# A two-layer transformer on one core: routed experts over all rows, or over sorted tiles of the rows that chose them

## The reference, cut to what matters

```
scores = softmax(x @ gate_w.T)                        # 8 experts
topk_w, topk_i = top_k(scores, 2)
topk_w = topk_w / sum(topk_w)
cw = zeros.at[token, topk_i].add(topk_w)              # 2 of 8 are not zero
g, u = x @ wg[e], x @ wu[e]                           # e of 8, 256 -> 128
eo = (silu(g) * u) @ wd[e]                            # 128 -> 256
y = sum over e of cw[:, e] * eo[e]
shared = (silu(x @ sg) * (x @ su)) @ sd               # 256 -> 256 -> 256
x = layernorm(x + y + shared)
```

## Time and profile before

| | us |
|---|---|
| median of 3 runs (794.51 to 799.8) | 799.59 |
| span of the profiled execution, core 0 | 798.3 |
| second attention's 8 items | 378.6 to 546.9 |
| tail | 546.9 to 798.3 |

### The profile page before, as it was taken

The page is one execution under the profiler, slowest core; times in us unless marked ns, Lnnn a source line. Parts: engine busy times, 40 slices in busy tenths (PEclk is TensorE's granted clock), DMA queues, the critical chain, the costliest instruction groups (busy, mean ns, idle before and its releaser), DMA issues.

```text
span 798.3 us, 10995 instructions
## 1 busy us (share of the span) xinstructions
PE 743.9 (93%) x3831; PEld 332.2 (42%) x3831; DVE 402.3 (50%) x984; ACT 395.3 (50%) x519; POOL 174.3 (22%) x194
## 2 busy tenths in 40 slices
PE   5998889999989789897999999989999999999996
PEld 2656222224323535342222222324466457448345
DVE  1578225334767787965133333465432842652525
ACT  1245858886778153453888888773121130120110
POOL 0012534443232222145244223231200200000000
PEclk9997789999999799999899999999999999999999
DMA  8401242332220000022444555470000000000000
GB/s 278 120 0 30 54 82 37 53 56 37 40 38 1 1 0 14 0 40 49 79 81 82 83 83 83 78 200 1 0 1 0 28 0 1 26 0 0 26 1 27
DMA packets 32276, 36.15 MB, mean 45 GB/s; under 512 B 7956, under 2 KB 21009, under 8 KB 32065
## 3 DMA queue, kind: packets, MB, share of 16 engines
q1 hardware_dynamic: 32217, 35.41, 21.7%
HBM read 12.54 MB, written 2.10 MB: 18 GB/s over the span
## 4 chain that ended last, share of the span: by engine, by line
PE 65%; DVE 13%; SPq 10%; ACT 5%; issue 4%; DMA 2%; POOL 1%; DVEq 0%; ACTq 0%; POOLq 0%
PE ps L2109 17%; PE ps L1303 13%; PE ps L1286 11%; PE ps L2134 9%; ACT probs L1373 3%; SPq L1024 3%; PE ps L1683 3%; SPq L999 2%; SPq L1031 2%; PE ps L400 2%; DVE stats L291 1%; PE ps L649 1%; PE ps L1670 1%; DVE raw L1206 1%; PE ps L2119 1%
## 5 line engine op out<-in xcount | busy, mean ns | idle before, releaser
L1373 ACT ACTIVATE probs<-ps 128x1024 f32<-128x1024 f32 (+1 forms) x320 | 276.0, 965 | 66.2 <-PE ps L1286 66.0
L1286 PE MATMUL ps<-ops_mem 99*128 99x512 bf16 (+3 forms) x768 | 167.5, 340 | 13.5 <-issue 6.7
L1303 PE MATMUL ps<-probs,vstat 128*32 128x512 f32 (+3 forms) x1536 | 168.9, 513 | 9.2 <-DVE raw L1206 7.4
L2109 PE MATMUL ps<-ops_mem,parts_mem 128*128 128x512 f32 x320 | 147.1, 605 | 1.0 <-DVE probs L2161 1.0
L1389 POOL TENSOR_SCALAR_AFFINE_SELECT probs<-probs 128x512 f32<-128x512 f32 x128 | 84.8, 663 | 223.1 <-ACT probs L1373 222.4
L1286 PEld LDWEIGHTS ps<-ops_mem 99*128 99x128 bf16 x768 | 58.1, 99 | 166.5 <-ACT probs L1373 86.1
L1206 DVE COPY raw<-ps 128x512 f32<-128x512 f32 x32 | 22.1, 691 | 167.4 <-PE ps L1303 167.2
L2055 ACT ACTIVATE ops_mem<-ps 128x512 f32<-128x512 f32 x40 | 23.9, 597 | 142.9 <-PE ps L2109 142.9
L2109 PEld LDWEIGHTS ps<-ops_mem,parts_mem 128*128 128x128 f32 x320 | 58.9, 191 | 68.4 <-issue 66.0
L2134 PE MATMUL ps<-parts_mem,probs 128*128 128x256 f32 x320 | 70.5, 380 | 0.0
L2134 PEld LDWEIGHTS ps<-parts_mem,probs 128*128 128x128 f32 x320 | 60.3, 190 | 8.4 <-issue 0.5
(11 more groups left out here) (191 smaller groups left out, 723.6 us busy)
## 6 DMA issues: line engine op xcount, KB each, us to landing
ops_mem<-parts_mem SPq DMA_DIRECT2D x276, 64.0 KB
ops_mem<-parts_mem SPq DMA_DIRECT2D x66, 32.0 KB
yT<-in_xT SPq DMA_DIRECT2D x4, 512.0 KB, 7.9
xres<-in_x SPq DMA_DIRECT2D x1, 2048.0 KB, 14.6
out<-ops_mem SPq DMA_DIRECT2D x3, 512.0 KB, 2.9
rope<-in_rope SPq DMA_DIRECT2D x1, 1024.0 KB, 6.8
parts_mem<-in_wg SPq DMA_DIRECT2D x2, 512.0 KB, 5.0
parts_mem<-in_wu SPq DMA_DIRECT2D x2, 512.0 KB, 6.9
```

What stands on the lines that cost most here:

```text
L1286: last = nc.tensor.matmul(ps[:, bank, o:o + CH - lo], kT[0:KDIM, buf, h if kh == GH else 0, kt * P:(kt + 1) * P], qT[0:KDIM, buf, h, c * C ...
L1303: last = nc.tensor.matmul(ps[32 * h:32 * h + 32, AV, lo:CH], vstat[:, i % 2, kt, h if kh == GH else 0, :], probs[:, s % PRING, h, 0:CH - l ...
L1373: nc.scalar.activation(o, banks, ACT.Exp, scale=score_scale).then_inc(s_exp, 1)
L2109: last = nc.tensor.matmul(ps[:, 4 + 2 * (e % 2) + m, :], w, xT[:, kk, :], start=kk == 0, stop=kk == 1)
```

## The change

Every token chose two experts, so a batch has 2048 (token, choice) pairs. The new tail sorts them by expert into 23 tiles of 128 slots (16 full ones and up to 7 more for the experts' partly filled last tiles), 46 for both batches.

- `Route` takes the place of `FirstChunk` and `Gates`. For a batch it makes the logits, softmax and the two highest, counts by a matmul with a triangle of ones how many earlier pairs chose the same expert (`rank`), and from it each pair's slot (`place`) and each tile's expert (`name_tiles`). For batch 0 (chunks 0 and 1: 4 half projections, 4 half transposes, logits of 8 tiles, rank) this is put beside items 4 to 7 of attention 1, for batch 1 into the first rounds of the tail.
- POOL scatters x to a DRAM tensor by slot: for each of 16 token tiles two indirect DMAs of 128 rows with 1 KB. Those DRAM tensors are filled with zeros during attention 0: after the stackings of items 2 and 3 SP issues a DMA of 3 MB each, from DRAM to DRAM.
- SP loads slot tiles back (ring of 6), PE transposes a tile, multiplies by gate and up weights side by side (256 columns), transposes the product, multiplies by the down weights; the expert's column is a register that PE loads from SBUF (`value_load`). SP stores the tile's result to DRAM, POOL gathers the two results of a token by indirect DMAs (32 in all), and DVE adds them, weighted, to x + shared. Gathers go through a ring of 4 token tiles.
- The tail works in rounds: in round r of a batch PE transposes tile r (`turn_x`), makes gate and up of tile r-1, transposes the product of tile r-2 and makes down of tile r-3; ACT follows with `keep_x(r)`, silu of r-1 and `keep_y(r-3)`, DVE with `keep_hT(r-2)` and `gated(r-1)`. There are 26 rounds in a batch.
- `load(j + 6)` stands behind `store(j)` on SP, which waits for `keep_y(j)`; `gather` waits for all stores of its batch and, from t = 4, for `add_routed(t - 4)`; the last loop over LAST takes tiles (0, 1), (2) and (3) of the last chunk.
- The shared expert is made by chunk, chunks 0 and 1 ahead of the tiles (with projections and transposes of chunks 2 and 3; in the excerpt below up of (1, 1), four half transposes and down of chunk 1 are left out), 2 and 3 at the end.

```diff
@@ attention, PE, DVE, POOL, SP of the second (and SP of the first) @@
+            def beside(self, pe, i, s):
+                if i == NI // 2 and s in (7, 8, 9, 10):
+                    self.project(pe, (s - 7) // 2, (s - 7) % 2)
+                if (i, s) in ((5, 4), (5, 8)):
+                    self.turn(pe, 0, (4, 8).index(s))
+                if (i, s) in ((5, 11), (6, 3)):
+                    self.turn(pe, 1, (11, 3).index(s))
+                if (i, s) == (6, 5):
+                    self.logits(pe, 0)
+                if (i, s) == (7, 2):
+                    self.rank(pe, 0)
+                    if layer == 1 and i == NI // 2:
+                        route.sum(dve, 0, 0)
+                        route.sum(dve, 0, 1)
+                        route.sum(dve, 1, 0)
+                        route.sum(dve, 1, 1)
+                        route.norm(dve, 0)
+                        route.apply(dve, 0)
...
                     take(dve, i, 1)
                 for i in range(2, NI):
                     ops.stack(sp, i)
+                    if layer == 0 and i in (2, 3):
+                        sp.dma_start(slot_x_of[i - 2].rearrange("(j p) n -> p j n", p=P),
+                                     a["none"].rearrange("p (j n) -> p j n", j=1).to_broadcast([P, SLOT_TILES, C])
+                                     ).then_inc(s_fill, 16)
@@ tail, SP @@
+                for b in range(NB):
+                    sp.wait_ge(s_scattered[b], 16 * 2 * TPB)
+                    lo, hi = b * SLOT_TILES, (b + 1) * SLOT_TILES
+                    for j in range(lo, lo + XR):
+                        load(j)
+                    for j in range(lo, hi):
+                        store(j)
+                        if j + XR < hi:
+                            load(j + XR)
@@ tail, POOL @@
+                outputs_there(pool, 2)
+                pool.wait_ge(ops[1].s_scores, NEXP * (NI - 1))
+                route.stage(2)
+                for t in range(TPB):
+                    scatter(t)
+                    if t == 2:
+                        outputs_there(pool)
+                        route.stage(3)
+                for t in range(TPB, 2 * TPB):
+                    scatter(t)
+                for t in range(2 * TPB):
+                    gather(t)
@@ tail, PE @@
+                def gate_up(j):
+                    b, n = j // SLOT_TILES, j % SLOT_TILES
+                    if n == 0:
+                        pe.wait_ge(route.s_tile, b + 1)
+                    at = pe.value_load(expert_of[b][0:1, n:n + 1], min_val=0, max_val=(EXPERTS - 1) * C)
+                    pe.wait_ge(s_xT, j + 1)
+                    for kk in range(2):
+                        last = nc.tensor.matmul(ps[:, bank(j), C:2 * C], slot_xT[:, j % 4, kk * P:(kk + 1) * P],
+                                                wgu[:, kk, bass.ds(at, C)], start=kk == 0, stop=kk == 1)
...
+                shared_up(0, 0)
+                route.project(pe, 2, 0)
+                route.project(pe, 2, 1)
+                shared_up(0, 1)
+                route.project(pe, 3, 0)
+                shared_down(0)
+                route.project(pe, 3, 1)
+                shared_up(1, 0)
...
+                for b in range(NB):
+                    for r, (j, j1, j2, j3) in rounds(b):
+                        if j is not None:
+                            turn_x(j)
+                        if j1 is not None:
+                            at[j1] = gate_up(j1)
+                        if j2 is not None:
+                            turn_h(j2)
+                        if j3 is not None:
+                            down(j3, at[j3])
+                        if (b, r) == (0, 0):
+                            route.logits(pe, 1)
+                        if (b, r) == (0, 7):
+                            route.rank(pe, 1)
+                        if (b, r) == (1, SLOT_TILES):
+                            shared_up(2, 0)
+                        if (b, r) == (1, SLOT_TILES + 1):
+                            shared_up(2, 1)
+                shared_down(2)
+                shared_up(3, 0)
+                shared_up(3, 1)
+                shared_down(3)
@@ tail, ACT @@
+                        if (b, r) == (0, 3):
+                            route.exp(act, 1)
@@ tail, DVE @@
+                        if b == 1 and r >= 8 and r % 2 == 0 and r < 24:
+                            add_routed((r - 8) // 2)
+                        if (b, r) == (1, 15):
+                            end(0, 0)
...
+                end(1, 1)
+                begin(2)
+                shared_gated(3, 0)
+                shared_gated(3, 1)
+                begin(3)
+                for t in range(2 * CT, 3 * CT):
+                    add_routed(t)
+                end(2, 2)
+                for t in range(3 * CT, 4 * CT):
+                    add_routed(t)
                 for n, (lo, hi) in enumerate(LAST):
...
+                    end(3 + n, 3, lo, hi)
```

More of the change, by code:

```diff
@@ L403, in project_y @@
             last.then_inc(s_proj, 1)
[L405 to L425 removed]
+        PICK_COUNT = 19
@@ new lines, in keep_turned, with logits @@
+            def keep_turned(self, eng, copy, m, kk):
+                eng.wait_ge(self.s_turned, 2 * m + kk + 1)
+                if m >= 2:
+                    eng.wait_ge(self.s_yst, NC)
+                copy(chunk_xT[m][:, kk, :], ps[:, self.BANK, :]).then_inc(self.s_xT, 1)
+            def logits(self, pe, b):
+                pe.wait_ge(self.s_xT, 4 * b + 4)
+                for m in range(2):
+                    for t in range(CT):
+                        for kk in range(2):
+                            o = 8 * (CT * m + t)
+                            last = nc.tensor.matmul(ps[:, self.BANK, o:o + 8],
+                                                    chunk_xT[2 * b + m][:, kk, t * P:(t + 1) * P],
+                                                    gatew[:, kk, :], start=kk == 0, stop=kk == 1)
+                last.then_inc(self.s_logit, 1)
@@ new lines, in rank @@
+            def rank(self, pe, b):
+                if b == 0:
+                    pe.wait_ge(self.s_table, 32)
+                pe.wait_ge(self.s_mask, b + 1)
+                nc.tensor.matmul(ps[:, self.BANK, 0:72], before_, mask[:, 0:72], start=True, stop=False)
+                for d in range(1, TPB + 1):
+                    last = nc.tensor.matmul(ps[:, self.BANK, 8 * d:72], ones_, mask[:, 0:72 - 8 * d],
+                                            start=False, stop=d == TPB)
+                last.then_inc(self.s_rank, 1)
@@ L1224, in _ @@
                 for i in range(NI):
-                    if layer == 1 and i == NI - 2:
-                        first.sum(dve)
                     if layer == 0 and i == NI - 1:
@@ L1331, in _ @@
                             ahead.beside(pe, i, s)
[L1332 to L1338 removed]
+                        if layer == 1:
+                            route.beside(pe, i, s)
                     if more:
@@ L1379, in _ @@
                 for i in range(NI):
-                    if layer == 1 and i == NI - 2:
-                        pool.wait_ge(s_y, NI)
-                        pool.wait_ge(s_vstat[layer], NI // 2)
-                        for g in range(NG // 2):
-                            first.stage(g, 0)
                     for d, s in enumerate(DIAG):
@@ new lines, in add_routed @@
+                def add_routed(t):
+                    b, m, n = t // TPB, t // CT, t % TPB
+                    dve.wait_ge(*s_begun(m + 1))
+                    dve.wait_ge(s_back[t % BR], 32 * (t // BR + 1))
+                    w = w_end[:, m, t % CT, :]
+                    for c in range(2):
+                        if c:
+                            dve.wait_ge(*s_sum(2 * t + 1))
+                        vec.scalar_tensor_tensor(out=w, in0=back[:, t % BR, c, :], scalar=gate[b][:, c, n:n + 1], in1=w,
+                                                 op0=ALU.mult, op1=ALU.add).then_inc(s_sum.sem, 1)
@@ L2304 @@
     bf16 = ml_dtypes.bfloat16
-    sel = np.zeros((32, EXPERTS, P), np.float32)
-    for part in range(3):
-        for e in range(EXPERTS):
-            sel[part * EXPERTS + e, e] = 1
     row = np.arange(P)
+    eight = np.arange(EXPERTS)
     perm = np.zeros((P, P), np.float32)
@@ L2355 @@
         "rope": _rope_tables(),
-        "sel": sel.astype(bf16),
+        "none": np.zeros((P, C), np.float32),
+        "before": np.concatenate([row[:, None] < row[None, :], np.ones((P, P), bool)], 1).astype(bf16),
+        "route": np.concatenate([np.tile(P * eight, 8), (eight[None, :] <= eight[:, None]).reshape(-1), np.arange(24)]
+                                ).astype(np.float32)[None],
         "iota8": np.arange(EXPERTS, dtype=np.float32)[None],
```

828 lines of the change are left out of this document (454 added, 374 removed).

## The result

The changed kernel takes 757.92 us (median of 4 runs, 755.33 to 762.57), the kernel before 799.69 beside it: ratio 0.950, 95% interval 0.945 to 0.955. The forecast was 766, range 738 to 806. The profiled execution has a span of 755.6 us.

What follows compares the result with a forecast made beforehand. PE was taken as the bound, busy 93% of the span and the tail its list of matmuls. Tail minus 43, attention plus 9, fill plus 1, together minus 33: span 765, forecast 766 us, range 738 to 806.

Steps and rivals of the forecast that it cites:

- What is removed, and PE's bare work: Tail: 181 of 251 us of expert work go; each slot tile costs PE 1.62 us, 46 of them 75 us.
- The round, 2.1 us: Slot-tile rounds in the tail: PE's work plus waits and register arithmetic, 2.1 us each, range 1.65 to 3.0.
- The four waits at 0.1: In each slot-tile round PE waits at four places, taken at 0.1 us each.
- the load ring: Slot-tile loads behind stores must land two rounds later: round at least 1.7 us with 2.2 landing, 2.35 with 3.5.
- rival 3: PE's clock falls to 1.2 GHz in the rounds: 1.62 us more a round, 840 us in all; chance 0.03.
- Rival 2: Register load not hidden, or dynamic address slows PE's issue: rounds of 3.0 us, 41 more, 807; chance 0.10.
- POOL's indirect DMAs: 64 scatters and gathers, taken at 1.5 us each, the middle between 0.34 to 0.7 and 2.36 us.
- its bounds of 1.67 and 1.8: Time per scatter, in us, up to which scatters stay hidden in the tail's first part and in batch 0.
- the 794: Total in us if POOL paid the page's whole indirect-DMA cost, 2.0 us plus bytes, all 64 times.
- Attention 1, plus 9: Second attention: routing work put beside it lengthens it by 9 us, range 5 to 16.
- it comes 1 to 1.5 us late each, 3.5: Second attention, items 4, 5 and 6: DVE's `take` is late behind queued routing steps, 3.5 us together.
- First part, gap, end, fill: Tail before the first round 34.5 us, gap between batches 3.4, end 47; zero fill in attention 0 plus 1.

Runs made afterwards that it cites:

- e4: Changed kernel with each slot tile's load issued once its buffer is turned, ahead of stores: 767.25 us, 5.5 less than e0.
- e10: Changed kernel with four edits: e3, e5, e4 with its gap fault addressed, and chunk 0's last norm in pieces: 731.48 us, ratio 0.918.
- e1: Changed kernel with each slot tile's expert a program constant, not a register load (wrong experts): 764.65 us, 8.1 less than e0.
- e2: Changed kernel with an added GpSimd addition of 0.62 us behind each of the 64 indirect DMAs: 772.87 us, ratio 0.968.
- e7: Changed kernel with the first batch's routing moved from the second attention to the start of the tail: 782.86 us, ratio 0.982.
- e11: Kernel of e10 with the routing norms of chunks 0 and 1 cut in two around item 5's outputs: 729.78 us, ratio 0.914.
- e9: Changed kernel with the 32 indirect scatters made plain DMAs (routed part wrong), gathers still indirect: 754.54 us, ratio 0.947.
- e6: Changed kernel with the DRAM slot arrays zero-filled twice in the first attention: 757.93 us, ratio 0.948.
- e0: The changed kernel itself, timed again on another chip: 772.75 us, ratio 0.969 against the kernel before.
- e3: Changed kernel with item 4's output copied and normalised before the routing's norm, and chunk 1 turned later in item 5: 768.78 us, ratio 0.964.
- e5: Changed kernel with its end reordered: 8 gather buffers, earlier additions of tiles 8 to 11, last chunk normed in two halves: 748.51 us, ratio 0.938.

## Why the prediction was right, and where not

**What is removed, and PE's bare work.** Right: 1.62 us a round from single instructions, 1.62 measured.

**The round, 2.1 us.** Too long. The 2.13 of batch 1 looks like it, but that is luck: it holds the 5.7 us of `end(0, 0)`, for which the sum had 4 us of its own. Beside the forecast's 2.1 stands 1.87, and 1.92 in batch 0 (51.5 us less the 9.3 that the sum had for logits, rank and routing, over 22 intervals). That is some 9 of the 12.5 us by which the tail is shorter than forecast. The four waits at 0.1 and the register's 0.1 aren't there in an undisturbed round. What is there is the other bound of that paragraph, the load ring: with a landing of 2.3 us, 0.5 + 0.7 + 2.3 over two rounds is 1.75 us, and I had not taken it into the value. e4 and e10 issue the loads earlier, and 1.62 is left. In e10 `end(0, 0)` is cut in pieces, and its 5.7 us are gone.

**The clock.** Of rival 3 little came: 0.94 and 0.91 over the two batches' rounds, with the lower level, 1.2 GHz, behind the gap and behind `end(0, 0)`, where gate and up take 1.91 us and not 1.03.

**The tensor load.** Rival 2 is out by e1; 46 of these loads measure 302 ns in the median. The page "DMA: Bandwidth & Descriptors" of the Trainium skill (Latency and other measured facts) gives such a load a floor of about 600 ns, and the trace disagrees.

**POOL's indirect DMAs.** Taken 1.5 us from bounds of 0.34 and 2.36, measured 1.28 and 1.32 with the pause. Eight gathers make 1.4 us of that in the end. What a slower GpSimd costs the sum had too low, and by the wrong way: at e2's period of 1.81 us its bounds of 1.67 and 1.8 and its 8 us per us at the end give 2.2 + 0.2 + 4.2 = 6.6 us over the changed kernel, and e2's tail is 16.7 longer. The way that I hadn't followed is `stage(3)`: the sum has a fixed 3 us for it and VectorE's norm together, but it stands behind six scatters. (The terms of that paragraph, 24 + 2.4 + 2 + 2.8, are also 31.2 and not 32.) The page "DMA: Bandwidth & Descriptors" of the Trainium skill (Anatomy of one DMA, SWDGE path) has a fixed 2.0 us plus the bytes; the 2.3 us for 128 KB, an estimate by it, are met by a scatter's landing, 2.4 us, and passed by a gather's, 3.1; GpSimd is free after 1.0 of it, so the 794 that came of charging GpSimd with all of it was too much.

**Attention 1, plus 9.** Too low: plus 14.4. The step that failed is "it comes 1 to 1.5 us late each, 3.5". I had counted VectorE's late copies as three equal small delays. There are two large ones, 6.2 us together: 3.64 us, where the whole norm of chunk 0 (6.5 us) stands ahead of `take`, and 2.60 where TensorE's transpose waits for chunk 1's norm, a waiter that I had not followed. The rest of the 5.4 us is work: TensorE's added 14.3 us for 12.9, and before's own work of this kind, which is worth 6.5 us (158.1 less e7's 151.6), where I had taken off 6.0 and 1.4. And a wait costs more than its length, for the granted clock is lower behind it: from the changed kernel to e11 the waits for VectorE fall from 8.1 us to 3.8, the time that the same 1186 matmuls keep PE busy from 161.65 us to 157.63 (clock 0.96 and 0.99), and the attention by 8.9.

**First part, gap, end, fill.** 32.5 for 34.5, with PE as the bound (e9: with plain scatters 31.9); the gap's wait 2.99 for 3.4, the end 45.6 for 47, by the chain that was forecast; the fill 0 for 1 (e6).

**The sum.** Tail 12.5 less than forecast, attention 5.4 more, what lies ahead 2.4 less: 755.6 for 765. Two errors stood against each other, a round that was too long and an attention that was too short; that the total is within 10 us is in part luck. The 772.75 us on e0's chip lie in the range, but no case of mine had their cause.

## What to carry to other kernels

Where a step is put beside a busy engine, follow each waiter of the engine that does it: what is queued behind the step there, and how long that can wait; if the step is longer than the time between two outputs, moving it only moves the wait (e3), and cutting it in pieces removes it, or most of it (e10, e11). Issue a ring's loads when their buffer is free and not behind the store of the same round. A chain at the end that reuses few buffers and norms the last piece alone is worth looking at first: 7.5 us came from four more buffers and an order of operations (e5). And follow what a slower engine holds back besides its own product: in e2 the scatters had slack, but a sum that stood behind six of them had none.

## What was not expected of the hardware

On one chip TensorE's semaphore signals reached VectorE and ScalarE 1 to 9.5 us late, by the profile's modelled ends, in some rounds in which GpSimd issued indirect DMAs, in four kernels of four; on other chips in none of nine. No wait of TensorE is put down to "remote" there, so ScalarE's and VectorE's own signals came on time. That the indirect DMAs bring it is argued from the coincidence, not shown: a run of e9 on that chip would tell. The kernel before, which has none, took 798.1 us on it as on the others.

A wait of TensorE was dearer than its length here: behind the 3.64 us at the end of item 4, and with the 2.60 near its own end, item 5 has a granted clock of 0.82 and takes 27.2 us; in e11, with waits of 0.3 us at most for the copies, it is 20.3 us at 1.00 (one turn of 0.66 us less in it).
